# The first stage of a signature, attention and expert kernel: stacked tails, the level-three sum as one f32 product, statistics by transposes

## What is computed

```python
C = Cin + 1                                   # 8 channels, time included
dx = jnp.transpose(x[:, 1:] - x[:, :-1], (1, 0, 2))
def step(levels, v):
    e = [v]
    for k in range(1, d):                     # d = 4
        e.append(_outer(e[-1], v) / (k + 1))
    new = []
    for k in range(d):
        acc = levels[k] + e[k]
        for i in range(k):
            acc = acc + _outer(levels[i], e[k - 1 - i])
        new.append(acc)
    sig = jnp.concatenate(new, axis=-1)       # 8 + 64 + 512 + 4096 numbers
    return (tuple(new), sig)
_, sigs = jax.lax.scan(step, init, dx)
h = jnp.transpose(sigs, (1, 0, 2)) @ W.T + b
xn = _layernorm(h)
q = _bn((xn @ Wq + bq).reshape(b * t, f), gq, betaq)   # mean and variance over all tokens
v = _bn((xn @ Wv + bv).reshape(b * t, DU * DK), gv, betav)
k = softmax over t of (xn @ Wk + bk)
```

## Time and profile before

| | |
|---|---|
| time, median of 3 runs | 776.1 us (768.93 to 781.59) |
| the profiled execution's own time | 769.51 us |
| its span, first to last instruction | 767.7 us |
| PE busy | 662.8 us (86%) |
| DVE busy | 476.0 us (62%) |
| ACT, POOL busy | 269.8 us (35%), 255.2 us (33%) |
| mean granted TensorE clock | 0.901 |

### The profile page before, as it was taken

One profiled execution on the slowest core, in us unless ns is written; L12 is line 12 of the kernel. 1 busy time (PEld: TensorE's weight loads), 2 busy tenths in 40 slices (PEclk: granted clock), 3 DMA queues, 4 the chain that ended last, 5 costly groups with the idle time before them and its releaser, 6 DMA issues. The chain is left out here.

```text
span 767.7 us, 13713 instructions
## 1 busy us (share of the span) xinstructions
PE 662.8 (86%) x4028; PEld 528.7 (69%) x4028; DVE 476.0 (62%) x1378; ACT 269.8 (35%) x592; POOL 255.2 (33%) x271
## 2 busy tenths in 40 slices
PE   1799999999999999982498978888989745999995
PEld 1588888888888888862266756666667543888894
DVE  7876666666666666666246556465565631777774
ACT  3222222222222222211236445544453612555552
POOL 5321122222223111101125465555455450333333
PEclk9999999999999999995558897988788965999998
DMA  8024555555554444445221222322222012222220
GB/s 230 0 71 130 164 160 159 160 160 160 160 166 137 140 138 138 141 148 123 100 96 50 69 90 79 106 83 83 77 73 83 23 48 64 57 62 70 71 64 9
DMA packets 88083, 79.37 MB, mean 103 GB/s; under 512 B 27782, under 2 KB 81117, under 8 KB 86886
## 3 DMA queue, kind: packets, MB, share of 16 engines
q1 hardware_dynamic: 84742, 72.53, 31.4%
q0 software_dynamic: 3296, 6.27, 2.6%
HBM read 31.24 MB, written 48.09 MB: 103 GB/s over the span
## 5 line engine op out<-in xcount | busy, mean ns | idle before, releaser
L918 DVE SCALAR_TENSOR_TENSOR P<-PS,QN 128x512 f32<-128x512 f32 x128 | 79.2, 681 | 51.1 <-PE PS L1037 51.1
L556 PE MATMUL PS<-Wh,Ah 128*126 128x512 f32 (+1 forms) x320 | 90.1, 411 | 2.2 <-ACT Ah L387 2.2
L556 PE MATMUL PS<-Wh,Al 128*126 128x512 f32 (+1 forms) x320 | 85.3, 396 | 0.0
L556 PE MATMUL PS<-Wl,Ah 128*126 128x512 f32 (+1 forms) x320 | 84.8, 395 | 0.0
L457 DVE SCALAR_TENSOR_TENSOR Z<-PS,Vt,Z 126x128 f32<-126x128 f32 x224 | 78.3, 349 | 7.2 <-PE PS L556 0.4
L556 PEld LDWEIGHTS PS<-Wh,Al 128*126 128x126 f32 (+1 forms) x320 | 59.9, 187 | 14.8
L556 PEld LDWEIGHTS PS<-Wl,Ah 128*126 128x126 f32 (+1 forms) x320 | 59.8, 187 | 14.5
L1191 POOL DMA_INDIRECT out_h<-OS,XS x39 | 37.9, 971 | 92.2 <-DVE OS L1235 91.7
L378 ACT ACTIVATE AS<-PS 128x504 f32<-128x504 f32 x32 | 18.9, 590 | 139.5 <-PE PS L585 139.5
L323 POOL TENSOR_TENSOR HB<-H,boutb 126x128 f32<-126x128 f32 x32 | 14.5, 454 | 156.3 <-DVE H L494 156.3
L556 PEld LDWEIGHTS PS<-Wh,Ah 128*126 128x126 f32 (+1 forms) x320 | 54.9, 187 | 16.4 <-issue 5.8
(11 more groups left out here) (214 smaller groups left out, 1565.0 us busy)
## 6 DMA issues: line engine op xcount, KB each, us to landing
routed<-nobody SPq DMA_DIRECT2D x30, 1170.0 KB, 5.1
IM<-v_pad SPq DMA_DIRECT2D x128, 78.8 KB
XS<-routed SPq DMA_DIRECT2D x39, 130.0 KB, 2.1
WRW<-in_w SPq DMA_DIRECT2D x16, 256.0 KB, 2.8
R<-h_rows SPq DMA_DIRECT2D x16, 129.9 KB
WR<-in_w SPq DMA_DIRECT2D x8, 256.0 KB, 3.1
q_raw<-QS SPq DMA_DIRECT2D x32, 63.0 KB
h_rows<-HB SPq DMA_DIRECT2D x32, 63.0 KB
```

What stands on the lines that cost most here:

```text
L556: ins = pe.matmul(psU[u][h].rearrange("p d o -> p (d o)"), a[0:rows, u, c], w[0:rows, c, h], start=(n == 0 and c == 0), stop=(n == 2 and c ...
L918: ins = dve.scalar_tensor_tensor(P[:, b, HV * h:HV * h + HV], psC[2 * pair + hb], 0.0, QN[:, g % 2, b:b + 1].broadcast_to([128, HV, SP]), ...
```

## The change

- **Tails.** The tail rows stand twice and in pieces in two operands `AT` of 128 rows (by 126 columns), with matching weights `WT`, so that the tail's three products become two matmuls. A half has 14 matmuls instead of 15. ACT builds the stacked rows in three copies (`tails`), PE turns them in two transposes, DVE makes their low parts in two instructions (64 and 8 partitions). The weights load has six blocks of 512 KB instead of five.
- **Level three.** `INC` is the moving operand of one f32 product of 512 columns (`third_sum`) with tokens on partitions; DVE adds `TOP` to it (`A3`), and PE transposes `A3` instead of `TOP`. `INC` has one buffer instead of two. ACT rounds from PSUM straight (`high_rows`); the copy of `TOP` and `AS` are gone.
- **Statistics.** `psQT` and `psVT` are transposes of the finished `QS` instead of products with the weights; their statistics are taken one step later, so the steps run to k = 34, and the two additions of a bias in `middle` go.
- **Level two in pieces.** `E2`, `E3` and the sums are made for 8 tiles at a time, pieces 1 to 3 in steps 0 and 1; POOL makes the first two `TOP` ahead of its low parts of W.
- **Banks.** `psU` has two banks instead of four: both tiles share one for each half. `Vt` is copied by ACT instead of DVE.

```diff
-        psU = [[PS[2 + 2 * u + h][0:TOK, :].rearrange("p (d o) -> p d o", d=4) for h in range(2)] for u in range(2)]
+        psU = [PS[2 + h][0:TOK, :].rearrange("p (d o) -> p d o", d=4) for h in range(2)]
...
+            def tails(t, u):
+                wait_from_one(act, at_done, t - 1)
+                for lo, hi, to, n in ((0, C2, 0, 2), (C2, TAIL, 2 * C2, 2), (C2, C2 + C, C2 + 96, 1)):
+                    part = A2X[:, bass.ds(t, 1), lo:hi]
+                    act.activation(AXs[:, u, to:to + n * (hi - lo)].rearrange("p (n c) -> p n c", n=n),
+                                   part.broadcast_to([TOK, n, hi - lo]), ACT.Copy).then_inc(ax_ready, 1)
+                wait_from_one(act, z_ready, t - 1)
+                act.activation(Vt[:, u], tile(V, t), ACT.Copy).then_inc(vt_ready, 1)
+            def high_rows(t, u):
+                act.wait_ge(tt_done, t + 1)
+                wait_from_one(act, u1_done, t - 1)
+                act.activation(Ah[:, u], psT, ACT.Copy).then_inc(ah_ready, 1)
+                act.wait_ge(at_done, t + 1)
+                act.activation(AT[:, u], psB, ACT.Copy).then_inc(ah_ready, 1)
...
+            def third_level(t, u):
+                dve.wait_ge(s3_done, t + 1)
+                dve.wait_ge(top_ready, t + 1)
+                wait_from_one(dve, tt_done, t)
+                dve.tensor_tensor(A3[:], psS3, TOP[:, u], ALU.add).then_inc(a3_ready, 1)
+            def low_rows(t, u):
+                dve.wait_ge(ah_ready, 2 * t + 1)
+                dve.tensor_tensor(Al[:, u], psT, Ah[:, u].bitcast(f32), ALU.subtract).then_inc(al_ready, 1)
+                dve.wait_ge(ah_ready, 2 * t + 2)
+                for lo, hi, c in ((64, 128, 0), (96, 96 + C, 1)):
+                    dve.tensor_tensor(AT[lo:hi, u, c], psB[lo:hi, c], AT[lo:hi, u, c].bitcast(f32), ALU.subtract).then_inc(al_ready, 1)
...
+            def third_sum(t):
+                pe.wait_ge(inc_ready, t + 1)
+                wait_from_one(pe, a3_ready, t)
+                pe.matmul(psS3, before, INC[:], start=True, stop=True).then_inc(s3_done, 1)
...
+                high_high = [(Ah[:, u, c], Wh[:, c, h]) for c in range(NCH)]
+                high_low = [(Ah[:, u, c], Wl[:, c, h]) for c in range(NCH)]
+                low_high = [(Al[:, u, c], Wh[:, c, h]) for c in range(NCH)]
+                tails = [(AT[:, u, 0], WT[:, 0, h]), (AT[0:96 + C, u, 1], WT[0:96 + C, 1, h])]
+                opening = isinstance(k, int) and k == 0 and h == 0
+                turn = high_high + low_high + tails[:1] + high_low + tails[1:] if opening else high_high + high_low + low_high + tails
...
                 if on(k, 0, NT):
                     pe.wait_ge(ah_ready, 2 * (k + 1))
-                    wait_from_one(pe, c0_done, k - 1)
+                    wait_from_one(pe, c0_done, k)
                     half(k, u, 0, u0_done)
...
-                    pe.matmul(psQT, wqkv_s[:, 0:F], XT[:, u], start=True, stop=True)
-                    pe.matmul(psVT, wqkv_s[:, F + DK:QKV], XT[:, u], start=True, stop=True).then_inc(qkv_done, 1)
...
+                if on(k + 2, 0, NT):
+                    third_sum(k + 2)
+                if on(k - 2, 0, NT):
...
+                    pe.wait_ge(qs_ready, k - 1)
+                    wait_from_one(pe, stats_done, k - 2)
+                    pe.transpose(psQT, QS[:, u, 0:F], ident_t)
+                    pe.transpose(psVT, QS[:, u, F + DK:QKV], ident_t).then_inc(qt_done, 1)
```

More of the change, by code:

```diff
@@ L218, in run_steps @@
         def run_steps(eng, step, after={}, extra=None, first=2):
-            for k in range(-1, 4):
+            for k in range(2 * first):
                 step(k, k % 2)
@@ L223, in run_steps @@
                     after[k]()
-            for k in range(4, 2 * first):
-                step(k, k % 2)
             if extra:
@@ L370, in step @@
+            act.wait_ge(consts_set, 3)
+            act.wait_ge(first_copies, 1)
+            act.wait_ge(a2_ready, 1)
+            tails(0, 0)
+            for c in (2, 3):
+                high(c, Wh[:, c])
+            high_rows(0, 0)
+            for c in range(2):
+                high(NCH + c, WT[:, c])
             def step(k, u):
+                w = 1 - u
                 if on(k + 1, 0, NT):
-                    wait_from_one(act, at_done, k)
-                    act.activation(AXs[:, 1 - u], A2X[:, bass.ds(k + 1, 1)].rearrange("p t c -> p (t c)"), ACT.Copy).then_inc(ax_ready, 1)
+                    tails(k + 1, w)
@@ L403, in w1_high @@
                                ACT.Copy).then_inc(w1_hi, 1)
-            run_steps(act, step, after={0: shared_high}, extra=w1_high, first=3)
+            run_steps(act, step, after={1: shared_high, 3: lambda: act.wait_ge(a2_ready, 8)}, extra=w1_high, first=3)
         @block.vector
@@ new lines, in _ @@
+            sums(0, 0)
+            dve.wait_ge(a2_ready, 1)
+            increments(0)
+            sums(0, 1)
+            increments(1)
+            third_level(0, 0)
+            second_level(1)
+            second_level(2)
+            low_rows(0, 0)
+            for c in range(BY_POOL, NCH):
+                weight_low(c)
+            dve.wait_ge(w_hi, NCH + 2)
+            dve.tensor_tensor(WT[0:TAIL, 1], raw[NCH + 1][0:TAIL], WT[0:TAIL, 1].bitcast(f32), ALU.subtract).then_inc(w_lo_dve, 1)
@@ new lines, in half @@
+            def half(k, u, h, done):
+                out = psU[h].rearrange("p d o -> p (d o)")
+                high_high = [(Ah[:, u, c], Wh[:, c, h]) for c in range(NCH)]
[4 more added lines that the diff above has]
+                turn = high_high + low_high + tails[:1] + high_low + tails[1:] if opening else high_high + high_low + low_high + tails
+                for n, (a, w) in enumerate(turn):
+                    if n == (4 if opening else 8):
+                        pe.wait_ge(al_ready, 3 * (k + 1))
+                    if opening and n == 8:
+                        pe.wait_ge(w_hi, NCH + 1)
+                    if opening and n == 9:
+                        pe.wait_ge(w_lo_pool, BY_POOL)
+                        pe.wait_ge(w_lo_dve, NCH - BY_POOL)
+                    if opening and n == 13:
+                        pe.wait_ge(w_lo_dve, NCH + 1 - BY_POOL)
+                    ins = pe.matmul(out, a, w, start=(n == 0), stop=(n == len(turn) - 1))
+                ins.then_inc(done, 1)
@@ L581, in step @@
                 if on(k + 1, 0, NT):
-                    pe.wait_ge(top_ready, k + 2)
-                    wait_from_one(pe, al_ready, k + 1)
-                    for c in range(NCH):
-                        ins = pe.transpose(psT[:, c], TOP[:, w, 128 * c:128 * c + 128], ident_t)
-                    ins.then_inc(tt_done, 1)
-                    pe.wait_ge(inc_ready, k + 2)
-                    pe.wait_ge(ax_ready, k + 2)
-                    for c in range(NCH):
-                        pe.matmul(psA[:, c], INC[:, w, 128 * c:128 * c + 128], before, start=True, stop=True)
@@ L591, in step @@
-                    if on(k - 1, 0, NT):
-                        pe.wait_ge(h_ready, k)
-                    pe.transpose(psB, AXs[:, w], ident_t).then_inc(at_done, 1)
+                    turn_rows(k + 1, w)
+                if on(k - 2, 0, NT):
+                    if isinstance(k, int) and k == 2:
+                        pe.wait_ge(small_in, 80)
+                    pe.wait_ge(xt_ready, k - 1)
+                    wait_from_one(pe, qs_ready, k - 2)
+                    pe.matmul(psQKV, XT[:, u], wqkv_s[:], start=True, stop=True).then_inc(qkv_done, 1)
@@ L604, in middle, with last_level @@
+            def last_level():
+                pe.wait_ge(a2_ready, 6)
+                level2(3)
+            run_steps(pe, step, after={0: second_levels, 1: last_level})
 def middle(nc, m):
```

361 lines of the change are left out of this document (179 added, 182 removed).

## The result

| | before | after |
|---|---|---|
| time, median | 774.02 us (4 runs) | 738.73 us (736.07 to 745.35, 4 runs) |
| ratio, 95% interval | | 0.9566 [0.9514, 0.9619] |
| profiled execution's own time, span | 769.51, 767.7 us | 736.07, 734.3 us |
| first stage ends at | 349.86 us | 320.27 us |
| from there to the end of the span | 417.8 us | 414.0 us |

The kernel is 4.3% faster; I had forecast 744 us in 734 to 758. The first stage is 29.6 us shorter, where I had worked out 28.9. But the parts of that sum did not all come out, and 3.8 us of the difference between the two profiled executions lie behind the first stage.

A forecast was written before the change was run, and what follows sets the result against it. PE's own queue was taken to bound the first stage. Savings of 24.1 + 2.5 + 1.0 + 1.3 = 28.9 us gave 740.6 from the profiled execution and 747.2 from the median; forecast 744 us, range 734 to 758.

The forecast's parts named there:

- PE's queue sets the first stage: First stage: PE is busy throughout, so an edit is worth what it takes from PE's queue.
- The step, 0.83 us shorter: Steps 2 to 31: PE's removed and added work gives 8.99 instead of 9.82 us, 24.1 us in all, bounds 17 and 31.
- the two statistics products less the two transposes: PE in each step: products of 0.31 + 0.32 us go, two transposes of `QS` at 0.107 each come.
- the bound of -0.60: Smallest gain per step in us: 0.23 more is paid for switches between the now smaller groups on PE.
- DVE keeps up: DVE in each step: chain of 7.24 of 8.99 us, 1.7 us left; rival that DVE or a hand-over binds, 0.09.
- The shared banks cost nothing: Halves waiting for the first or second `combine` in each step: over 2.5 us of cover, so nothing was charged.
- Ahead of step 2, 2.5 us sooner: Start of the first stage: step 2 begins near 43.5 us; bounds 6 sooner to 1.5 later.
- The last step and the end, 2.3 us: Step 31 and the last stores: second half ends 1.0 us sooner, q, k, v behind it 1.3 sooner.
- The sum, 28.9: Whole kernel, in us: 24.1 from the steps, 2.5 ahead of step 2, 1.0 and 1.3 at the end.
- The time, 744: Whole kernel: 744 us, taken between 740.6 from the profiled execution and 747.2 from the median of three runs; forecast chance 0.70.
- The second stage gives something back: Rival, second stage: a stretch at the 1.2 GHz level longer by 20 us costs 10, giving 754 us; chance 0.08.
- The clock in the first stage: Rival: more transposes and waits before W's low parts lower PE's clock, a step then costing about 17.5 us; chance 0.03.

The follow-up runs named there:

- e1_fifteenth: The changed kernel with a fifteenth large matmul in each half again, the first product made twice; 751.5 us, ratio to before 0.970.
- e2_products: The changed kernel with the statistics of q and v made by products with the weights again instead of transposes of `QS`; 759.6 us, ratio to before 0.984.
- the load test: The changed kernel with two or four more DVE instructions of 126 x 512 per step; 749.9 us with two, 794.7 us with four.
- e5_poolfree: The changed kernel with POOL's two subtractions for the low parts of W replaced by clearing them; 730.5 us, ratio to before 0.946.
- v2_order: The changed kernel with five DVE instructions, pieces of `E2` and `E3`, moved behind the low parts of tile 1; 737.4 us, ratio to before 0.959.
- the two second profiles: The changed kernel and the kernel before, each run again unchanged for another profile; 741.5 and 773.6 us, first stages ending at 322.3 and 349.0 us.

## Why the prediction was right or wrong, point by point

- **PE's queue sets the first stage: right.** One added matmul costs what it takes (e1_fifteenth), and 28 large matmuls, clock and lack of idle brackets are as forecast.
- **The step, 0.83 us shorter: the mechanism right, the size too small.** It was 0.97 over steps 2 to 31. The 1.00 of the running steps has in it that the last of them makes no level three (0.03). Mis-sized terms: the two statistics products less the two transposes, 0.42 in the sum, 0.56 by e2_products, mostly because q, k, v itself drops from 0.27 to 0.16 when a half follows it instead of another f32 product; `psH`, for which I had charged no change, 0.32 to 0.22 from its new place. I had put the switches between groups on the cost side only (the bound of -0.60); they came out on the other. Against that the two large matmuls are 0.44, not 0.48, and the tails cost more: I had charged 0.107 for the second transpose and left the first at its 0.03, but both take 0.11, so that they add 0.19. The two transposes of `QS` (0.107 each) and level three (0.90 to 0.86) were right. Last, in the kernel before, the transpose of `XN` cost 0.03 in one step and 0.10 to 0.30 in most of those between, 0.08 on average; now it is 0.03 in all. This gain of 0.05 was in no term, and what makes it was not tested.
- **DVE keeps up: right, with less room.** Its chain was put at 7.24 us and is 8.85 - 1.55 = 7.30. The room was put at 1.7, its idle bracket is 1.55, and the load test gives 1.15.
- **The shared banks cost nothing: right as far as seen.** No idle bracket of PE stands before a first half in running steps. A kernel with the shared banks alone was not tried.
- **Ahead of step 2, 2.5 us sooner: wrong, 0.74 later**, within the bounds I gave (6 sooner to 1.5 later). I had DVE's low parts ready at about 25 and 18.4 us from there to step 2; it was 26.64 and 20.1. Two steps failed. The first puts the two pieces of `E2` ahead of the low parts of tile 0 at the price that they have alone, while the low parts of W behind them were priced with POOL beside them. The pieces took 5.01 us; the low parts of W then took 4.52 + 1.21 instead of 7.88, which gave a part back. I had read that contention in the earlier trace rows for `Vhalf` and `Wl` and had it removed in one place without asking where POOL's 5 us would fall now. The second takes PE at full pace behind the low parts: it had just waited 3.22 us and ran at a granted clock of 0.50 until about 30 us, 1.7 us lost. e5_poolfree (5.4 us less without POOL's two instructions, and 18.5 us behind the low parts, nearly the 18.4 of the sum) and v2_order (2.1 us less by order alone) show both. The inputs, 0.95 us later (4.91 against 3.96), are in the 26.64: without that the start would be 0.2 us shorter than before.
- **The last step and the end, 2.3 us: right** by the first two profiles, 2.3: 1.2 to the end of the second half, where I had 1.0, and 1.1 behind it, where I had 1.3. By the two second profiles it is 1.1 (18.4 against 17.3).
- **The sum, 28.9: right for partly wrong reasons.** The steps gave 28.0 instead of 24.1 and the start took 0.7 instead of giving 2.5; the two errors nearly cancel to 29.6, and that is luck.
- **The time, 744 for 738.7.** The base was chosen between 769.5 and 776.1, and the median of before came out at 774.0, so the base is not what was off. The medians of whole executions lie 32 to 35 us apart, and the stages of the profiles 26.7 to 29.6. The stages behind give 410.8 to 425.3 us in thirteen profiles, on average 416.9 in the two of before and 417.7 in the eleven with the new first stage, so no gain is seen there. The rest of some 5 us is about as large as the interval of the ratio (0.5% of 774 is 4 us), and whether anything but chance is in it stays open.
- **The second stage gives something back: did not come.** Behind the first stage it was 414.0 and 417.6 us in the two profiles of the changed kernel, 417.8 and 415.9 in those of before.
- **The clock in the first stage: the rival came only at the start.** With nine transposes a step instead of six it stayed at 1.00 in the running steps. Where PE stood before the low parts of W, which the rival names too, it fell to 0.50 and cost the 1.7 us above; it also fell in the second profile of before (0.66 on average from 26 to 31 us), and step 2 began no later for it (45.90). The rule of the Trainium skill that transposes do not count as activity ("TensorE: Matmul & The Clock Gate", Part 4) is not put to the test by that, since the large matmuls between them fill 6.7 of the 8.85 us of each step.

## What to carry to other kernels

Where one engine's queue sets the time, what an instruction costs depends on its neighbour: price a removed instruction together with the borders it leaves, and measure it by adding it back once. An idle bracket is an upper bound on free time; the load test gave three quarters of it, with a price of the test itself in the missing quarter. And when a change moves work away from one contention, look for where the other engine's long instruction falls now: here a two-input instruction of GpSimd made two of VectorE's take four times as long, and moving them behind other work gave back 2.1 of the 5.4 us. A wait that it leaves on PE can cost twice, once as idle time and once more at the lower clock behind it.

## What the runs showed of the hardware that I had not expected

- A large matmul (512 columns, at clock 1.00) costs 0.222 us when one is added to a row of 14, while the mean over a half with its borders is 0.239.
- A small f32 product with no other f32 product next to it costs 0.16 to 0.22 us from start to start, and 0.27 to 0.32 with one before or behind it, also where a row of large matmuls stands on its other side.
- VectorE's two-input instruction on SBUF went from 0.64 to 2.5 us each beside a two-input instruction of GpSimd, ending 0.55 us behind it. It was not slowed beside a memset of GpSimd or where one input came from PSUM.
- The running step was equal to 0.001 us (8.823) in six profiles; what scatters in this kernel are the start, step 2 and the stages behind, where the granted clock changes from run to run.
